# The main trip of a fused GNN and expert layer in another order on three engines

## Chip, cores and metric

One core of a Trainium2 chip. The metric is the device time of one execution in microseconds (us). The kernel before took 1512.84 us, the median of three runs (1510.32 to 1513.54).

## What is computed

The reference, cut to what matters:

```python
def layer(x, src, dst, W, b, gate_w, gate_b, w1, b1, w2, b2):   # x: 6250 x 256, 100000 edges sorted by dst
    h = layernorm(x)
    agg = segment_sum(h[src], dst) / max(degree, 1)
    out = concat([h, agg]) @ W                                   # 512 x 256
    x = x + out / norm(out) + b
    h = layernorm(x)
    probs = softmax(h @ gate_w + gate_b)                         # 8 experts
    idx, prb = argmax(probs), max(probs)
    pos = position of the node in its expert's list              # running count, in node order
    kept = pos < C                                               # C = 977
    y = relu(buf[e] @ w1[e] + b1[e]) @ w2[e] + b2[e]             # 256 -> 1024 -> 256, on the kept rows
    return x + nan_to_num(y[idx, pos] * prb * kept)
```

## The kernel before, in words

The nodes are cut into 49 blocks of 128. The edges, sorted by destination, are cut into 196 quads of 512 (four tiles of 128). A first stage (to about 135 us) normalises x, splits each value into three bf16 parts, and writes them to DRAM (`parts_d`). Then comes the main loop of 49 trips, each with four quads. The main loop is followed by trips without quads, which finish the last nodes and the last chunks of experts.

**Edge work, four times in each trip.** GpSimd (POOL) gathers the quad's source rows, one indirect DMA for each tile, into `ring`, which has room for two quads (`gather`, L460). VectorE (DVE) makes the 0/1 matrix `sel` of 128 edges by 128 nodes for four tiles (`select_quad`, L991). TensorE (PE) multiplies `sel` by the gathered rows into PSUM `ps_q` (`visit`, L684 and L690: a *visit* is four tiles for one block). DVE adds the sum of the visit before to `acc` (`add_last`, L1000). A quad that crosses from one block to the next has two visits. Since 128 nodes have some four quads of edges, there is about one such crossing in each trip, in any of its four quads.

**Node work, once in each trip, for one block.** ACT and DVE write [normalised x, mean of neighbours] to `cat` (`prepare_node`); PE transposes it (L725), ACT copies it to `cat_t` (L580), PE multiplies by the GNN weights (`linear`, L738), ACT takes the norm (L591, L515 to L517), DVE makes the new row and its mean and variance (`new_row`, L856 to L1113), then the factors of the second normalisation (`normalise_row`, L1118 to L1121). ACT normalises it (L613) and PE transposes it (`xl_transposes`, L774). In the next trip PE makes the eight gate logits (`gate`, L780), DVE chooses the expert (`route`, L1128 to L1154), PE counts the choices (`counts`, L789 and L790), and DVE works out the row's slot (`finish_row`, L1072 to L1090, which ends with the semaphore `row_ready`). POOL then scatters `row` to `disp_d`, ordered by experts (`dispatch`, L470).

**Chunk work, once in each trip from the ninth on.** It takes 128 dispatched rows of one expert through its two layers: `xc_transposes` (L731), `up` in two halves (L747), ACT's copy to `hid` (L598), `hid_transposes` (L755), ACT's relu (L604), `down` as eight products (L766), and DVE's `result` (L1210 to L1231). POOL scatters the result to the output (`results`, L478).

**What sets the order.** No scheduler does: each engine runs its own program in the order in which it is written, and semaphores tie them. On PE a table `plan` says which piece of node or chunk work follows tile 0, 1, 2 and 3 of each quad's last visit. On DVE the order is the text of its `trip`; a helper `chains` runs several dependent sequences in step, with a drain between steps. POOL's trip is the sixteen gathers of its four quads, then `dispatch`, then `results`:

```python
for k in range(QS):
    for half in range(2):
        if quads: gather(t, k, half)      # waits ring_free: the quad two before has been read
if prev:  dispatch(t, rows)               # waits row_ready >= t + 1
if chunk: results(t)                      # waits res_ready
```

The first and last node blocks of each quad (eight numbers for each trip) lie in `qtab`, and are loaded into registers once a trip: on DVE at L1252, behind the selection of quad 3, on PE at L720, behind tile 0 of quad 3.

## Time and profile before

| | |
|---|---|
| median of three runs | 1512.84 us |
| span of the profiled execution, first to last instruction | 1742.4 us |
| mean granted TensorE clock in it | 0.898 of full speed |
| busy in it: PE / PE weight loads / DVE / ACT / POOL | 1183.2 / 838.8 / 898.6 / 469.4 / 922.7 us |
| main loop, first eight trips (no chunk work) | about 135 to 351 us |
| main loop, the other 41 trips | about 351 to 1561 us |
| trips without quads | about 1561 to 1742 us |

The profiled execution has no time of its own beside its span, and this is 15% above the median of the runs. Busy is the time that an engine had an instruction in hand; PE's ends are modelled. Every row of the trace below is in the time of the profiled execution.

### The profile page before, as it was taken

How to read it: one execution, taken by the hardware profiler on the slowest of the kernel's cores; microseconds unless marked ns; L12 is line 12 of the kernel's file. 1: busy time of each engine (PE TensorE's matmuls, PEld its weight loads, DVE VectorE, ACT ScalarE, POOL GpSimd, SP SyncE). 2: the span in 40 equal slices, each digit the busy share in tenths (PEclk: the TensorE clock that was granted, in tenths of full speed). 3: DMA queues.
4: the chain of work that ended last, by engine and by line, in shares of the span. 5: the costliest groups of instructions: out<-in, count | busy, mean ns of one | idle time of the engine just before them, and what ended most of it. 6: DMA issues, size and time to landing. Idle time of an engine off the chain costs nothing.

```text
span 1742.4 us, 32300 instructions
## 1 busy us (share of the span) xinstructions
PE 1183.2 (68%) x6813; PEld 838.8 (48%) x6814; DVE 898.6 (52%) x3823; ACT 469.4 (27%) x1362; POOL 922.7 (53%) x939
## 2 busy tenths in 40 slices
PE   0105566677777777777777776877677777777785
PEld 0004444455555555555555554645455655554553
DVE  5753444455555545454555554554555545554443
ACT  2221111122222222222222322223222222233432
POOL 4136656656666656555656655565556665640110
PEclk9998676789999989998989998999998899888998
DMA  7736667554545444544445444444454544431111
GB/s 236 235 134 205 185 215 232 185 160 131 147 136 146 135 131 132 149 121 134 136 118 139 126 138 115 134 127 140 114 143 121 146 120 137 124 103 34 38 42 38
DMA packets 126810, 238.77 MB, mean 137 GB/s; under 512 B 21263, under 2 KB 85126, under 8 KB 126792
## 3 DMA queue, kind: packets, MB, share of 16 engines
q0 software_dynamic: 55808, 160.87, 32.7%
q1 hardware_dynamic: 70984, 77.72, 14.1%
q14 instruction: 14, 0.11, 0.0%
q8 instruction: 4, 0.07, 0.0%
HBM read 207.46 MB, written 39.29 MB: 142 GB/s over the span
## 4 chain that ended last, share of the span: by engine, by line
PE 28%; issue 19%; DVE 17%; another core or an unknown queue 11%; DVEq 10%; DMA 7%; ACT 4%; POOL 2%; SPq 2%; ACTq 0%; POOLq 0%
PE ps_q L684 10%; PE ps_h L747 5%; PE ps_b L766 5%; PE ps_a L738 3%; DVEq L1252 3%; DVEq L1060 2%; DMA ring<-parts_d,idx 2%; DVE sel L991 2%; PE ps_a L725 2%; DMA b_b<-in_L_ffn_b 2%; DMA out<-ys,node_i 1%; PE ps_t L755 1%; DVE acc L1000 1%; ACT cat_t L580 1%
## 5 line engine op out<-in xcount | busy, mean ns | idle before, releaser
L460 POOL DMA_INDIRECT ring<-parts_d,idx x784 | 763.0, 973 | 541.1 <-PE ps_q L684 277.9
L684 PE MATMUL ps_q<-ring,sel 128*128 128x256 bf16 x2928 | 506.0, 299 | 245.0 <-DMA ring<-parts_d,idx 96.7
L684 PEld LDWEIGHTS ps_q<-ring,sel 128*128 128x128 bf16 x2928 | 270.4, 106 | 416.8 <-issue 242.2
L766 PE MATMUL ps_b<-w_sb,hid_t 128*128 x864 | 264.6, 441 | 124.2 <-issue 71.2
L991 DVE SCALAR_TENSOR_TENSOR sel<-lane,block,dst_t 128x512 bf16<-128x512 bf16 x245 | 184.4, 753 | 197.4 <-issue 116.2
L766 PEld LDWEIGHTS ps_b<-w_sb,hid_t 128*128 128x128 f32 x864 | 169.6, 214 | 161.6 <-issue 141.5
L747 PE MATMUL ps_h<-w_sb,hid_t 128*128 x432 | 213.6, 622 | 5.7 <-ACT hid_t L583 5.7
L1000 DVE TENSOR_TENSOR acc<-acc,ps_q 128x257 f32 x245 | 103.3, 422 | 178.3 <-issue 57.3
L690 PE MATMUL ps_q<-ones_bf,sel 128*128 128x1 bf16 x976 | 170.8, 175 | 0.0
L738 PE MATMUL ps_a<-gw_sb,cat_t 128*128 128x256 f32 x416 | 136.3, 459 | 19.3 <-ACT cat_t L580 15.6
L604 ACT ACTIVATE hid_t<-ps_t,b_t 128x128 f32<-128x128 f32 x432 | 117.8, 382 | 55.5 <-remote 40.1
L515 ACT ACTIVATE sm<-sm 128x1 f32<-128x1 f32 x104 | 21.1, 203 | 358.3 <-DVE sm L1113 192.0
L690 PEld LDWEIGHTS ps_q<-ones_bf,sel 128*128 128x128 bf16 x976 | 105.0, 108 | 21.0
L478 POOL DMA_INDIRECT out<-ys,node_i x55 | 57.2, 1041 | 108.6 <-DVEq L1060 94.9
L598 ACT ACTIVATE hid<-ps_h 128x512 f32<-128x512 f32 x108 | 62.5, 596 | 193.7 <-PE ps_h L747 142.1
L470 POOL DMA_INDIRECT disp_d<-row,slot x53 | 60.2, 1136 | 90.9 <-issue 53.1
L747 PEld LDWEIGHTS ps_h<-w_sb,hid_t 128*128 128x128 f32 x432 | 76.3, 195 | 66.2 <-issue 65.2
L738 PEld LDWEIGHTS ps_a<-gw_sb,cat_t 128*128 128x128 f32 x416 | 84.0, 223 | 35.3 <-ACT cat_t L580 20.5
L755 PE MATMUL ps_t<-ident,hid 128*128 128x128 f32 x432 | 69.5, 284 | 30.0 <-ACT hid L598 25.7
L755 PEld LDWEIGHTS ps_t<-ident,hid 128*128 128x128 f32 x432 | 46.8, 141 | 46.0 <-ACT hid L598 33.3
L580 ACT ACTIVATE cat_t<-ps_a 128x512 f32<-128x512 f32 x52 | 31.0, 597 | 129.8 <-remote 64.7
L591 ACT ACTIVATE hid_t<-ps_a 128x256 f32<-128x256 f32 x52 | 19.9, 383 | 161.6 <-PE ps_a L738 91.4
(180 smaller groups left out, 1296.1 us busy)
## 6 DMA issues: line engine op xcount, KB each, us to landing
w_sb<-in_L_ffn_w SPq DMA_DIRECT2D x32, 512.0 KB
ring<-parts_d,idx POOLq DMA_INDIRECT x784
disp_d<-row SPq DMA_DIRECT2D x1, 8450.0 KB
parts_d<-w_sb SPq DMA_DIRECT2D x6, 1344.0 KB, 5.8
xs<-disp_d SPq DMA_DIRECT2D x55, 130.0 KB
ys<-disp_d SPq DMA_DIRECT2D x55, 130.0 KB
b_b<-in_L_ffn_b SPq DMA_DIRECT2D x55, 128.0 KB
xb<-in_x SPq DMA_DIRECT2D x51, 128.0 KB
```

What stands on the lines that cost most here:

```text
L460: pool.indirect_dma_start(ring[:, (k % 2) * TQ + j, :], None, parts_d[:, :], bass.IndirectOffsetOnAxis(ap=idx[:, k * TQ + j:k * TQ + j + 1 ...
L470: pool.indirect_dma_start(disp_d[:, :], bass.IndirectOffsetOnAxis(ap=slot[0:rows, 0:1], axis=0), row[0:rows, :], None, bounds_check=EX * S ...
L598: act.activation(hid[:, h * 512:(h + 1) * 512], ps_h[:, h * 512:(h + 1) * 512], ACT.Copy).then_inc(hid_ready, 1)
L604: done = act.activation(hid_t[:, j, :], ps_t[:, j, :], ACT.Relu, bias=b1_t[:, ds(e * JF + j, 1)])
L684: mm = pe.matmul(ps[:, 0:D], sel[:, s, j, :], ring[:, (k % 2) * TQ + j, part * D:(part + 1) * D], start=(j == 0 and part == 0), stop=(j == ...
L690: mm = pe.matmul(ps[:, D:AW], sel[:, s, j, :], ones_bf[:, :], start=False, stop=(j == TQ - 1), skip_group_check=True)
L738: last_ = pe.matmul(ps_a[:, 0:KD, :], cat_t[:, k, :], gw_sb[:, k, :], start=(k == 0), stop=(k == 2 * KD - 1))
L747: last_ = pe.matmul(ps_h[:, h * 512:(h + 1) * 512], xc_t[:, k, :], w1_sb[:, k, ds(expert[0] * F + h * 512, 512)], start=(k == 0), stop=(k ...
L755: last_ = pe.transpose(ps_t[:, j, :], hid[:, j * P:(j + 1) * P], ident[:, :])
L766: last_ = pe.matmul(ps_b[:, 0:D], hid_t[:, j, :], w2_sb[:, j, ds(expert[0] * D, D)], start=(j == 0), stop=(j == JF - 1))
L991: dve.scalar_tensor_tensor(out=sel[:, s, :, :], in0=lane[:, :].rearrange("p (j m) -> p j m", j=1).to_broadcast((P, TQ, P)), scalar=block0[ ...
L1000: dve.tensor_tensor(to, to, ps_q[s][:, 0:AW], ALU.add).then_inc(acc_done, 1)
```

## The change

Nothing is computed otherwise. Five things are done to the main trip.

1. PE's `plan`: `linear` (both halves), `up` 0, `up` 1 and the second half of `down` now stand behind tile 3 of quads 0, 1, 2 and 3. The `cat` transposes stand behind the gate, `xl_transposes` behind tile 1 of quad 3, `hid_transposes` 1 beside it. The trips without quads have a list of their own.
2. The loads of `qtab`: on PE behind `up` 0, into a second set of registers that is copied at the end of the trip; on DVE in two halves, behind the first step of `result` and behind the selection of quad 3.
3. DVE's trip: the logits come first of all; `new_row` comes before the sum of quad 2, `normalise_row` behind the selection of quad 3, and only then the rest of `result` with `finish_row`.
4. ACT's trip follows: the exponential of the gate comes first, relu and the copies of `hid` alternate (`hid` now holds one half), and the next node's `cat` and the copy of the normalised transposes stand at the end.
5. ACT copies `row` to a buffer `drow` when the dispatch before has landed, and POOL scatters `drow`. `new_row` no longer waits for that dispatch.

```diff
@@ gpsimd @@
-                    disp_d[:, :], ...(ap=slot[0:rows, 0:1], axis=0), row[0:rows, :], None,
+                    disp_d[:, :], ...(ap=slot[0:rows, 0:1], axis=0), drow[0:rows, :], None,
@@ scalar: the end of a trip @@
+                if chunk:
+                    hid_copy(0)
                 if node:
                     act.wait_ge(stat2_ready, t + 1)
                     act.activation(cat[:, D:2 * D], row[:, 0:D], ...).then_inc(xl_ready, 1)
+                if chunk:
+                    relu(0)
+                    hid_copy(1)
+                if node:
+                    act.wait_ge(xl_ps, t + 2)
+                    act.activation(cat_t[:, 0:KD, :], ps_a[:, 0:KD, :], ACT.Copy).then_inc(xlt_ready, 1)
+                if chunk:
+                    relu(1)
+                if node and next_node:
+                    prepare_node(t + 1, block_of(t + 1, next_known))
+                if node:
+                    act.wait_ge(disp_out, 16 * (t + 1))
+                    act.activation(drow[:, :], row[:, :], ACT.Copy).then_inc(drow_ready, 1)
@@ tensor @@
+                plan = [[steps((prev, gate), (node, cat_transposes)),
+                         steps((chunk, load_expert)),
+                         steps(),
+                         steps((node, linear, 0), (node, linear, 1))],
+                        [steps((chunk, xc_transposes)),
+                         steps(),
+                         steps(),
+                         steps((chunk, up, 0), (True, load_quads))],
+                        [steps((prev, counts)),
+                         steps((chunk, hid_transposes, 0)),
+                         steps(),
+                         steps((chunk, up, 1))],
+                        [steps(),
+                         steps((chunk, hid_transposes, 1), (node, xl_transposes)),
+                         steps((chunk, down, (0, 1, 2, 3))),
+                         steps((chunk, down, (4, 5, 6, 7)), (True, turn_quads))]]
@@ vector @@
-                dve.wait_ge(disp_out, 16 * (t + 1))
...
             def trip(...):
+                logits, routed = route(t) if prev else ([], [])
+                chains(logits)
                 if quads:
                     dve.wait_ge(cat_ready, t + 1)
                     add_last(t, 0)
                     select_quad(t, 1)
-                chains(route(t) if prev else [], choose(t, whole=prev) if chunk else [])
+                chains(routed, choose(t, whole=prev) if chunk else [])
                 if quads:
                     add_last(t, 1)
                     select_quad(t, 2)
-                chains(result(t, node) if chunk else [],
-                       ([nothing] * 3 if chunk else []) + finish_row(t) if prev else [])
+                take_y, rest = result(t, node) if chunk else (nothing, [])
+                take_y()
+                if quads:
+                    dve.load(regs[0:4], qtab[0:1, ds(t * QS + QS, QS // 2), :])
+                if node:
+                    new_row(t)
                 if quads:
                     add_last(t, 2)
                     select_quad(t, 3)
-                    dve.load(regs, qtab[0:1, ds(t * QS + QS, QS), :])
+                    dve.load(regs[4:8], qtab[0:1, ds(t * QS + QS + QS // 2, QS // 2), :])
                 if node:
-                    new_row(t)
+                    normalise_row(t)
+                else:
+                    dve.drain()
+                chains(rest, finish_row(t) if prev else [])
                 if quads:
                     add_last(t, 3)
-                if node:
-                    normalise_row(t)
-                if quads:
                     select_quad(t + 1, 0)
```

Where the rows of two engines now stand. In the rows, `[waits ...]` names the semaphores that a row waits for; ISA and REGISTER_ALU rows work on registers.

DVE at the start of a trip with chunk work. Before, behind the selection of quad 1:

```order
L991 ISA [waits visit_done]
L991 SCALAR_TENSOR_TENSOR sel<-lane,block,dst_t 128x512
L1128 TENSOR_TENSOR g<-ps_b,gateb_sb 128x8 [waits logit_ps]
L1165 SCALAR_TENSOR_TENSOR g<-seen,taken 1x8
L1131 TENSOR_REDUCE sm<-g 128x1
```

Of the change, at the head of the loop:

```order
L1308 UNCONDITIONAL_BRANCH
L1308 ISA
L1159 TENSOR_TENSOR g<-ps_b,gateb_sb 128x8 [waits logit_ps]
L1162 TENSOR_REDUCE sm<-g 128x1
L1066 ISA [waits cat_ready]
L1067 ISA [waits visit_done]
L1032 TENSOR_TENSOR acc<-acc,ps_q 128x257
```

The wait for the gate's logits moved ahead of quad 1's sum and selection.

DVE where `finish_row` begins (`g<-ps_b,seen`, which waits `count_ps`). Before, right behind the selection of quad 2 and the start of `result`:

```order
L991 SCALAR_TENSOR_TENSOR sel<-lane,block,dst_t 128x512
L1208 REGISTER_ALU [waits cat_ps]
L1209 REGISTER_ALU [waits y_ready]
L1210 TENSOR_TENSOR b_b<-ps_b,b_b 128x256 [waits ys_in]
L1213 TENSOR_SCALAR b_b<-b_b,ys 128x256
L1217 TENSOR_SCALAR cat<-b_b 128x256
L1218 TENSOR_TENSOR cat<-b_b 128x256
L1221 TENSOR_TENSOR cat<-cat 128x256
L1072 TENSOR_TENSOR g<-ps_b,seen 128x8 [waits count_ps]
```

Of the change, behind `new_row`, quad 2's sum and quad 3's selection:

```order
L1023 SCALAR_TENSOR_TENSOR sel<-lane,block,dst_t 128x512
L1290 ISA
L1290 TENSOR_LOAD qtab
L888 SCALAR_TENSOR_TENSOR sm<-sm 128x1 [waits ln2_ready]
L890 TENSOR_SCALAR sm<-sm 128x1
L1149 TENSOR_SCALAR sm<-sm 128x1
L1151 TENSOR_TENSOR row<-sm 128x1
L1152 TENSOR_TENSOR row<-sm 128x1
L1245 TENSOR_SCALAR b_b<-b_b,ys 128x256
L1104 TENSOR_TENSOR g<-ps_b,seen 128x8 [waits count_ps]
```

`finish_row` moved down by `new_row`, one sum, one selection and `normalise_row`.

POOL at the end of its trip, of the change; before, the same rows stand there with `row` for `drow` (L460 to L478):

```order
L464 DMA ring<-parts_d,idx 128x768 [waits ring_free]
L464 DMA ring<-parts_d,idx 128x768
L472 REGISTER_ALU [waits x1_out]
L474 DMA disp_d<-drow,slot 8320x260 [waits row_ready]
L480 REGISTER_ALU
L482 DMA out<-ys,node_i 6250x256 [waits res_ready]
```

Nothing moved on POOL: the next trip's first gather still stands behind both scatters.

## Rows read from the trace of the kernel before

**Rows 1.** The page: the chain that ended last, by engine.
```profile
PE 28%; issue 19%; DVE 17%; another core or an unknown queue 11%; DVEq 10%; DMA 7%; ACT 4%; POOL 2%; SPq 2%; ACTq 0%; POOLq 0%
```

**Rows 2.** Register loads by line: duration ns min/median/max, first and last start us.
```profile
L1252 DVEq TENSOR_LOAD <-qtab x49: 1457/1878/2031, 155.5 to 1551.4; - x49
L720 PEldq TENSOR_LOAD <-qtab x49: 1949/1967/2218, 156.5 to 1552.5; - x49
```

**Rows 3.** Waits in 371:1558 us: engine, line, releaser: us, times, longest.
```profile
POOL ring L460 <- PE ps_q L684: 228.5, 128, 2.7
...
PE ps_b L766 <- issue: 71.2, 42, 4.1
```

**Rows 4.** Timeline, ACT and then PE: start us, us, what [idle before <-releaser].
```profile
815.19 1.14 ACT L604 ACTIVATE hid_t<-ps_t,b_t 128x128 f32<-128x128 f32 x4 [6.65 <-remote]
...
808.60 0.66 PE L755 MATMUL ps_t<-ident,hid 128*128 128x128 f32 x4 [1.25 <-issue]
```

**Rows 5.** Timeline of DVE and POOL, 930.7 to 937 us: slot, scatters, next gathers.
```profile
930.78 0.16 DVE L1090 TENSOR_TENSOR slot<-sm 128x1 int32<-128x1 f32 x1
...
931.86 1.02 POOL L470 DMA_INDIRECT disp_d<-row,slot  x1 [0.93 <-DVE slot L1090]
...
934.49 1.17 POOL L460 DMA_INDIRECT ring<-parts_d,idx  x1 [0.30 <-issue]
935.97 1.06 POOL L460 DMA_INDIRECT ring<-parts_d,idx  x1 [0.31 <-issue]
```

**Rows 6.** Timeline: a gather (POOL) and PE's visit that waited for it.
```profile
959.56 0.94 POOL L460 DMA_INDIRECT ring<-parts_d,idx  x1 [0.30 <-DVE slot L1090]
...
962.68 0.50 PE L684 MATMUL ps_q<-ring,sel 128*128 128x256 bf16 x3 [0.30 <-DMA ring<-parts_d,idx]
```

**Rows 7.** Timeline of PE: the gate, and part of `down`.
```profile
940.04 1.11 PE L766 MATMUL ps_b<-w_sb,hid_t 128*128 x4
...
944.00 0.50 PE L684 MATMUL ps_q<-ring,sel 128*128 128x256 bf16 x3 [0.81 <-issue]
...
944.36 0.59 PE L780 MATMUL ps_b<-gatew_sb,cat_t 128*128 128x8 f32 x4
...
965.98 1.61 PE L766 MATMUL ps_b<-w_sb,hid_t 128*128 x4 [1.79 <-issue]
```

**Rows 8.** Timeline of DVE, 948 to 971 us: one trip's pieces.
```profile
948.24 0.16 DVE L1128 TENSOR_TENSOR g<-ps_b,gateb_sb 128x8 f32<-128x8 f32 x1
...
949.16 0.16 DVE L1135 RECIPROCAL sm<-sm 128x1 f32<-128x1 f32 x1 [0.40 <-issue]
...
951.94 0.42 DVE L1000 TENSOR_TENSOR acc<-acc,ps_q 128x257 f32 x1
...
953.55 0.42 DVE L1210 TENSOR_TENSOR b_b<-ps_b,b_b 128x256 f32<-128x256 f32 x1
...
957.19 0.17 DVE L1072 TENSOR_TENSOR g<-ps_b,seen 128x8 f32<-128x8 f32 x1 [1.41 <-remote]
...
959.32 0.16 DVE L1090 TENSOR_TENSOR slot<-sm 128x1 int32<-128x1 f32 x1
...
960.38 0.75 DVE L991 SCALAR_TENSOR_TENSOR sel<-lane,block,dst_t 128x512 bf16<-128x512 bf16 x1 [0.32 <-issue]
...
961.78 0.75 DVE L991 SCALAR_TENSOR_TENSOR sel<-lane,block,dst_t 128x512 bf16<-128x512 bf16 x1 [0.31 <-issue]
963.87 0.22 DVE L856 SCALAR_TENSOR_TENSOR sm<-sm 128x1 f32<-128x1 f32 x1 [1.34 <-issue]
...
966.74 0.15 DVE L1113 TENSOR_SCALAR sm<-sm 128x1 f32<-128x1 f32 x1
...
970.19 0.21 DVE L856 SCALAR_TENSOR_TENSOR sm<-sm 128x1 f32<-128x1 f32 x1
...
970.90 0.15 DVE L1121 TENSOR_TENSOR row<-sm 128x1 f32<-128x1 f32 x1
```

**Rows 9.** A stretch of the trace: us, busy by engine, granted clock, DMA.
```profile
966.50:969.80 3.30, 3.30 (x11) 2.32 (x10) 0.34 (x3) 0.40 (x2) 1.67 (x2) 0.50 0.78 203
```

More of the change, by code:

```diff
@@ L104, in gnn_moe_layer @@
         row = sb("row", [P, ROW], FP32)
+        drow = sb("drow", [P, ROW], FP32)
+        lim_t = sb("lim_t", [P, D], FP32)
         slot = sb("slot", [P, 1], I32)
@@ L414, in _ @@
             pool.memset(xb[:, :], 0.0)
+            pool.memset(drow[:, :], 0.0).then_inc(drow_ready, 1)
             pool.memset(ones_bf[:, :], 1.0).then_inc(pool_step, 1)
@@ L470, in dispatch @@
                 pool.indirect_dma_start(
-                    disp_d[:, :], bass.IndirectOffsetOnAxis(ap=slot[0:rows, 0:1], axis=0), row[0:rows, :], None,
+                    disp_d[:, :], bass.IndirectOffsetOnAxis(ap=slot[0:rows, 0:1], axis=0), drow[0:rows, :], None,
                     bounds_check=EX * SLOTS - 1, oob_is_err=False).then_inc(disp_out, 16)
@@ L559, in prepare_node, with block_of, trip, hid_copy @@
                                ).then_inc(cat_ready, 1)
-            def trip(t, node=True, prev=True, chunk=True, known=None):
-                c = chunks(t)
-                if node and known is None:
-                    act.load([blk], ntab[0:1, ds(t, 1)])
-                    known = act.snap(blk, min_val=0, max_val=NB - 2)
+            def block_of(t, known):
+                if known is None:
+                    act.load([blk], ntab[0:1, ds(t, 1)])
+                    return act.snap(blk, min_val=0, max_val=NB - 2)
+                return known
+            def trip(t, node=True, prev=True, chunk=True, next_node=True, next_known=None):
+                c = chunks(t)
+                e = None
+                def hid_copy(h):
+                    act.wait_ge(hid_ps, 2 * c - 1 + h)
+                    act.activation(hid[:, :], ps_h[:, h * 512:(h + 1) * 512],
+                                   ACT.Copy).then_inc(hid_ready, 1)
+                def relu(h):
+                    act.wait_ge(hidt_ps, 2 * c - 1 + h)
+                    for j in range(h * 4, h * 4 + 4):
+                        done = act.activation(hid_t[:, j, :], ps_t[:, j, :], ACT.Relu,
+                                              bias=b1_t[:, ds(e * JF + j, 1)])
+                    done.then_inc(hidt_ready, 1)
                 if prev:
-                    act.wait_ge(xl_ps, t + 1)
-                    act.activation(cat_t[:, 0:KD, :], ps_a[:, 0:KD, :], ACT.Copy).then_inc(xlt_ready, 1)
+                    act.wait_ge(logit_ready, t + 1)
+                    act.activation(g8[:, 1, :], g8[:, 0, :], ACT.Exp, bias=sm[:, 16:17],
+                                   accum_out=sm[:, 17:18]).then_inc(exp_ready, 1)
                 if node:
-                    prepare_node(t, known)
+                    act.wait_ge(cat_ps, t + 1)
+                    act.activation(cat_t[:, :, :], ps_a[:, :, :], ACT.Copy).then_inc(catt_ready, 1)
                 if chunk:
@@ L718, in load_quads, with turn_quads @@
                 def load_quads():
-                    pe.load(regs, qtab[0:1, ds(t * QS + QS, QS), :])
+                    pe.load(next_regs, qtab[0:1, ds(t * QS + QS, QS), :])
+                def turn_quads():
+                    for now, then in zip(regs, next_regs):
+                        pe.reg_mov(now, then)
                 def cat_transposes():
@@ new lines, in trip @@
+                        [steps(),
+                         steps((chunk, hid_transposes, 1), (node, xl_transposes)),
+                         steps((chunk, down, (0, 1, 2, 3))),
+                         steps((chunk, down, (4, 5, 6, 7)), (True, turn_quads))]]
+                alone = steps((prev, gate), (chunk, load_expert), (node, cat_transposes), (chunk, xc_transposes),
+                              (node, linear, 0), (node, linear, 1), (chunk, up, 0), (chunk, up, 1), (prev, counts),
+                              (chunk, hid_transposes, 0), (chunk, hid_transposes, 1), (node, xl_transposes),
+                              (chunk, down, tuple(range(JF))))
@@ L818, in trip @@
+                if quads:
+                    for k in range(QS):
                         quad(t, k, plan[k])
-                    else:
-                        for step in plan[k]:
-                            step()
+                else:
+                    alone()
             pe.load(regs, qtab[0:1, 0:QS, :])
@@ L1310, in _ @@
                 dve.reg_add(t_reg, t_reg, 1)
-            chains(result(dve.snap(t_reg), False))
+            take_y, rest = result(dve.snap(t_reg), False)
+            chains([take_y] + rest)
 _INS = ["x", "src", "dst", "L0_gnn_weight", "L0_gnn_bias", "L0_ffn_gate_w", "L0_ffn_gate_b",
```

71 lines of the change are left out of this document (23 added, 48 removed).

## Prediction

> **What bounds the kernel now.** I read the views in this order: the chain that ended last, the waits, then the timelines of single trips. The chain has no owner [rows 1]: PE has 28% of it, DVE with its queue 27%, and 19% is "issue", time without a visible cause. So the question is in which loop of dependences a trip closes. The main loop has 41 trips with chunk work, and they take 29.5 us each in the profiled execution ((1561 - 351) / 41, from the table).
>
> The profiled execution is 230 us longer than the median run. I read why in PE's completions: the transposes of 808.60 us and 0.66 us have released ACT only at 815.19 [rows 4], though nothing that the trace shows held PE. The matmul stood still, and engines behind it show "remote" waits. Such gaps come with the many records of PE, so I take them as made by the recording. The durations of DVE, POOL and the DMAs are not of that kind, and the sum below rests on them. Of the 230 us I give 12 to the stages outside the 41 trips, which then have 520 of their 532 us; the 41 trips have 1512.84 - 520 = 993 us without the recording, **24.2 us each**. The sum is made against this, and so against the median.
>
> Three things are near 24.2 us. POOL issues 16 gathers of 0.94 and 0.30 us between them [rows 6], and two scatters of 1.3 us, 22.5 us in all [rows 5]. It had to wait for PE to free the ring for 228.5 us in 40 trips, 5.7 us a trip [rows 3], so it runs ahead. DVE has about 23 us of work and overheads in a trip. PE has some 19 us at full clock, and stalls.
>
> **The change part by part.**
>
> *The loads.* PE's load of eight registers takes 1.97 us [rows 2], and `down` waits behind it for most of the 71.2 us that its "issue" row shows [rows 3], 1.7 us a trip. Behind `up` 0, whose four passes keep PE busy for about 1.8 us, it is nearly hidden: up to -1.7 us for PE. On DVE the load takes 1.88 us, of which 1.34 us is idle time before L856 [rows 2, 8]. Two halves of 0.94 us each, behind instructions of 0.42 and 0.75 us, leave 0.73 and 0.40 us: -0.2 us. No row has a load of four registers; between nothing saved by halving (1.88 us each, +1.7 us) and two halves fully hidden (-1.3 us) I take half the time for half the registers. The Trainium skill ("Runtime: NRT & Kernel Launch", Instruction fetch mechanics) gives such a load about 200 ns a register; the trace has 235 ns, and by the page's figure the two halves would cost 0.3 us less a trip and the total would be 11 us lower.
>
> *The long products at the end of each quad.* When a quad crosses into a new block, DVE's selection and sum stand between two visits; it now has 1.8 to 1.9 us of products beside it. That is a gain of at most 1.5 us a trip for PE, again only if PE or DVE sets the end.
>
> *The later dispatch.* This is what decides. POOL's order is not changed: gathers of trip t, dispatch, results, and only then the first gather of trip t + 1. The dispatch waits for `row_ready`, the end of `finish_row`. Before, this comes early: behind quad 2's selection. Now `new_row`, a sum, a selection, half a load and `normalise_row` stand ahead of it. And DVE's trip now begins with the wait for the gate, which PE makes behind tile 0 of quad 0, which needs the first gather. That closes a loop: slot written, dispatch, results, gather, landing, tile 0, gate, all of DVE's trip up to the slot.
>
> From the slot to the landed tiles [rows 5, 6]: slot's end 930.94 to the dispatch's start 931.86, 0.92 us; both scatters, to the next gather's start at 934.49, 2.63 us; two gathers, to 937.03, 2.54 us; landing, from a gather's end at 960.50 to the visit at 962.68, 2.18 us. Sum **8.3 us**.
>
> From the landed tiles to the slot:
> - tile 0 and gate [rows 7]: 944.00 to 944.95, and 0.1 us to DVE: 1.05 us
> - logits, route and choose [rows 8]: 948.24 to 951.94 less 0.40 us of waiting is 3.30 us. The two logit steps now run alone and the nine steps of `choose` follow; two short rounds more, 0.5 us: 3.80 us
> - three times sum and selection (quads 1, 2, 3), 951.94 to 953.55 each [rows 8]: 4.83 us
> - first step of `result`, 0.42 and a drain: 0.52 us
> - first half of the load, as above: 0.73 us
> - `new_row`, 963.87 to 966.89 [rows 8]: 3.02 us
> - second half of the load: 0.40 us
> - `normalise_row`, 970.19 to 971.05 and a drain [rows 8]: 0.96 us
> - rest of `result` with `finish_row`: 953.55 to 959.48 less the 1.41 us of waiting is 4.52 us; less the first step (0.52) and the last, behind the slot (0.6): 3.40 us
>
> Sum **18.7 us**, and the loop has 27.0 us. A crossing in quad 1, 2 or 3 adds a selection and a sum, 961.78 less 960.38, 1.4 us [rows 8]. A crossing in quad 0 adds more: the extra visit comes ahead of the gate and needs the other half of the quad, two gathers (2.5 us) and two tiles more (0.7 us), 3.2 us. With one crossing a trip the mean is 1.85 us: **28.9 us a trip**, against 24.2. PE, after the slot, has only `down` (four products in 1.9 us twice, by 1.11 us for two with overlap [rows 7]) and tile 3, about 4.2 us, so it stands still for some 4 us until the tiles land.
>
> The same account of the kernel before: slot at about 11 us of the trip instead of 19, so the loop has some 21 us, and does not bind. POOL is then ahead.
>
> *What goes with it.* DVE's wait for the last dispatch is gone (the trace shows it at nothing). ACT's copy to `drow` costs 0.6 us on an engine that is busy for 27%, and comes when the scatter has landed, 5 us after the slot, ahead of the 9 us at which ACT is next needed. ACT's relu 0 and second copy of `hid` now wait for `normalise_row`; PE's `down` waits for the slot anyway. All of these: nothing. The memset of `drow`: below 1 us, once. In the first eight trips, without `result` and the second scatter, the loop has about 24.5 us, under the 27 us that they take now: nothing, with 10 us kept for the range. The trips without quads have the same pieces in nearly the same order: nothing, within 10 us.
>
> **Sum.** 41 x (28.9 - 24.2) = 193 us, and 1512.84 + 193 = **1705 us**.
>
> The pauses also touch PE's clock. After 1.79 us without a matmul, PE has the lower of its two levels, 1.2 GHz, in 966.5 to 969.8 us (granted 0.50), and two products of `down` take 1.61 us and not 1.11 [rows 7, 9]. The Trainium skill ("TensorE: Matmul & The Clock Gate", What's actually happening) says that the throttled state is the default and that activity lifts it. By that rule tile 0 and the gate, behind a pause of 4 us each trip, would take about twice their 0.95 us, and the total would be near 1740.
>
> **The rivals.**
>
> *The ends of PE decide (faster).* If the slot came soon enough for the gathers to land by the time PE has finished `down`, PE would keep its 1.7 us from the load and part of the crossing, until DVE's 23 us and POOL's 22.5 bind: 1 us a trip, 1470 us. It decides if slot to landing (8.3 us) is no longer than the 4.2 us of PE work behind the slot, so DVE would have to reach the slot 4 us earlier than the rows say, or do its trip in 20 us less waits. For it speaks the "issue" row of `down` and that every stall named in it is on PE; against it, the fixed order of POOL. Chance 0.14.
>
> *The late completions are real in every run (a small loss).* Then all of the profile shrinks alike, by 1512.84 / 1742.4 = 0.868, and the before has 29.5 us a trip in it. The new loop has 28.9 and perhaps 2 us of late completions in it: (30.9 - 29.5) x 0.868 x 41 = 50 us, 1563 us. For it: the profile cannot tell which of its gaps the recording made. Chance 0.2.
>
> *No difference.* PE's gain and the longer loop cancel, or DVE bound both: 1513 us, chance 0.04.
>
> **How the numbers follow.** The forecast has a chance of 0.62, and its own range is 1640 to 1765: 1 us a trip either way for the cut of the rounds, the loads and the clock. The range for 8 in 10 goes from 1560, which takes in the rival of a small loss, to 1765. It leaves out the two cases at or below 1513 and a little at each end. A measurement of this kernel can tell about 0.2% (3 us) from no change. Faster by more: 0.14. Within it: 0.04. Slower by more: 0.82.
>
> **What would show it.** Right: POOL waits for DVE's slot (L1122) before the dispatch in every trip, and no longer for PE to free the ring; PE's largest wait is for the gathered tiles, some 4 us at tile 0 of quad 0, once a trip; DVE waits at the logits at the head of its trip; slot to slot is about 29 us. `down` has no "issue" wait any more. Wrong: if POOL still waits for the ring most of the time, or if PE goes from `down` straight to the next trip's tile 0, the loop does not bind.

## The result, and the profile after

The changed kernel takes **1794.18 us** in the median (1788.50 to 1795.93, 4 runs), the kernel before beside it 1511.58 us (1509.12 to 1513.54, 4 runs): 1.186 times the time, 95% interval 1.182 to 1.190, 283 us more. The forecast was 1705 us, and its range ended at 1765: the sign and the place were right, the size was not, by 89 us.

The experiments were run in five rounds, each on one chip and each with the kernel before beside them. In four of the rounds that kernel takes 1738 to 1748 us in the median, and I call these *long* rounds. In the fifth it takes 1516.79 us, and beside the result 1511.58: these are *short*. (The expectations say "a chip of 1740 us" and "a chip of 1512 us"; the last section comes back to whether it is the chip.) The profile of before has a span of 1742.4 us, as in a long round; the profile after was taken in a short one (1795.93 us, span 1793.7). So rows of before and of after can't be laid side by side for PE's ends; for DVE, POOL and the DMAs they can. Medians below are of all runs of a kernel in its round; ratios, with 95% intervals, use only the runs within 1.5% of the kernel's fastest.

The page of the changed kernel: its span, the chain that ended last by engine and by line, and two groups of section 5 (line engine op, names, count | busy, mean ns | idle before it, and what ended most of it):

```profile
span 1793.7 us, 32491 instructions
...
issue 23%; DVE 22%; DMA 17%; PE 15%; DVEq 12%; POOL 6%; ACT 3%; SPq 1%; POOLq 1%; ACTq 0%
...
L795 PE MATMUL ps_b<-w_sb,hid_t 128*128 x864 | 218.5, 400 | 0.6 <-issue 0.6
L1159 DVE TENSOR_TENSOR g<-ps_b,gateb_sb 128x8 f32<-128x8 f32 x53 | 8.8, 167 | 373.6 <-PE ps_b L809 373.6
```

In the chain of before [rows 1] PE had 28% and DMA 7%. Now DMA and POOL have 23% together, and PE 15%: the chain goes through the gathers. `down` (L795) has lost its "issue" wait of 71.2 us [rows 3], as the load of PE's registers stands elsewhere.

The waits of the main loop, 371 to 1600 us (39 trips of chunk work; engine, line, releaser: us in total, times, longest):

```profile
POOL disp_d L474 <- DVEq L1092: 327.9, 40, 9.6
DVE g L1159 <- PE ps_b L809: 315.4, 39, 8.7
...
PE ps_q L709 <- DMA ring<-parts_d,idx: 197.2, 46, 5.6
...
PE ps_t L784 <- ACT hid L577: 105.2, 78, 1.9
```

POOL hardly waits for PE to free the ring (27.4 us in all, 228.5 before [rows 3]). It stands at the dispatch for 8.2 us in every trip. Its releaser is named DVEq L1092, which is DVE's queue at the head of `finish_row`; what the dispatch waits for is `row_ready`, the slot of L1122, and it starts 0.91 to 0.92 us behind the slot's end in each of 40 trips (ninth to forty-eighth). DVE stands at the logits 8.1 us a trip, PE at the gathered tiles some 5 us. Three engines wait once a trip, each for the next: a ring.

One turn of it, from POOL's timeline, 998 to 1030 us (start us, us, line, what, [idle before <-releaser]):

```profile
998.58 1.01 POOL L474 DMA_INDIRECT disp_d<-drow,slot  x1 [8.69 <-DVEq L1092]
999.90 1.31 POOL L482 DMA_INDIRECT out<-ys,node_i  x1 [0.30 <-issue]
1001.51 0.99 POOL L464 DMA_INDIRECT ring<-parts_d,idx  x1 [0.31 <-issue]
1002.81 0.96 POOL L464 DMA_INDIRECT ring<-parts_d,idx  x1 [0.30 <-issue]
...
1029.43 1.02 POOL L474 DMA_INDIRECT disp_d<-drow,slot  x1 [7.81 <-DVEq L1092]
```

and from the timeline of PE and DVE in the same turn:

```profile
1006.72 0.82 PE L709 MATMUL ps_q<-ring,sel 128*128 128x256 bf16 x3 [4.69 <-DMA ring<-parts_d,idx]
...
1007.40 1.00 PE L809 MATMUL ps_b<-gatew_sb,cat_t 128*128 128x8 f32 x4
...
1008.45 0.17 DVE L1159 TENSOR_TENSOR g<-ps_b,gateb_sb 128x8 f32<-128x8 f32 x1 [7.76 <-PE ps_b L809]
...
1021.91 0.75 DVE L1023 SCALAR_TENSOR_TENSOR sel<-lane,block,dst_t 128x512 bf16<-128x512 bf16 x1 [1.99 <-PE ps_q L715]
...
1028.37 0.15 DVE L1122 TENSOR_TENSOR slot<-sm 128x1 int32<-128x1 f32 x1
```

This turn takes 1029.43 less 998.58, 30.85 us. Over the 41 trips with chunk work it is 31.27 us in the mean: L1159 starts at 349.10 us in the ninth trip and at 1600.03 in the forty-ninth, 40 trips later. 41 of these are 1282 us, so the rest of the program has 512 us. With about as much outside the loop in the kernel before, its trips take (1511.6 - 512) / 41 = 24.4 us where it runs in 1512 us; that is an estimate, as no trace shows that kernel in a short round.

The granted clock in three stretches of this turn (us, PE busy and its instructions, PEclk, DMA, GB/s): `down`, the pause, and tile 0 with the gate.

```profile
999.80:1002.10 2.30, 2.23 (x13) 1.00 0.05 11
1002.10:1006.70 4.60, 0.00 (x0) 0.88 0.62 179
1006.70:1009.00 2.30, 2.28 (x12) 0.50 0.60 172
```

Behind the pause of 4.7 us PE has the lower of its two levels, 1.2 GHz; tile 0 takes 0.82 us where it took 0.50, and the gate 1.00 where it took 0.59 [rows 7].

### The profile page after: what moved, and what is told of

It reads as the page before. It is cut to its first block, busy times and chain, and to the rows that moved or that the text cites. A ratio compares the mean times of both kernels' runs of the same rounds, so it can differ in the third digit from the quotient of the medians.

```text
span 1793.7 us, 32491 instructions
## 1 busy us (share of the span) xinstructions
PE 1170.5 (65%) x6813; PEld 856.1 (48%) x6814; DVE 893.6 (50%) x3823; ACT 478.3 (27%) x1414; POOL 913.6 (51%) x940
## 3 DMA queue, kind: packets, MB, share of 16 engines
q1 hardware_dynamic: 70984, 77.72, 13.2%
## 4 chain that ended last, share of the span: by engine, by line
issue 23%; DVE 22%; DMA 17%; PE 15%; DVEq 12%; POOL 6%; ACT 3%; SPq 1%; POOLq 1%; ACTq 0%
DMA ring<-parts_d,idx 13%; PE ps_q L709 7%; DVEq L1092 3%; DVEq L1290 2%; DVE sel L1023 2%; PE ps_b L809 2%; POOL ring L464 2%; DVEq L1284 2%; DMA b_b<-in_L_ffn_b 2%; PE ps_t L784 2%; POOL out L482 2%; PE ps_a L767 1%; ACT hid L577 1%; DMA out<-ys,node_i 1%; PE ps_b L795 1%
## 5 line engine op out<-in xcount | busy, mean ns | idle before, releaser
L464 POOL DMA_INDIRECT ring<-parts_d,idx x784 | 750.9, 958 | 259.6 <-issue 221.7
L1023 DVE SCALAR_TENSOR_TENSOR sel<-lane,block,dst_t 128x512 bf16<-128x512 bf16 x245 | 184.4, 752 | 196.2 <-PE ps_q L715 114.0
L474 POOL DMA_INDIRECT disp_d<-drow,slot x53 | 54.3, 1025 | 433.5 <-DVEq L1092 390.5
L795 PE MATMUL ps_b<-w_sb,hid_t 128*128 x864 | 218.5, 400 | 0.6 <-issue 0.6
L1159 DVE TENSOR_TENSOR g<-ps_b,gateb_sb 128x8 f32<-128x8 f32 x53 | 8.8, 167 | 373.6 <-PE ps_b L809 373.6
L795 PEld LDWEIGHTS ps_b<-w_sb,hid_t 128*128 128x128 f32 x864 | 162.2, 197 | 26.4 <-issue 1.3
L784 PE MATMUL ps_t<-ident,hid 128*128 128x128 f32 x432 | 71.6, 289 | 133.9 <-ACT hid L577 133.9
L767 PE MATMUL ps_a<-gw_sb,cat_t 128*128 128x256 f32 x416 | 124.6, 451 | 0.0
L784 PEld LDWEIGHTS ps_t<-ident,hid 128*128 128x128 f32 x432 | 46.6, 142 | 156.1 <-ACT hid L577 151.4
L482 POOL DMA_INDIRECT out<-ys,node_i x55 | 66.0, 1199 | 108.0 <-DVEq L1092 94.3
L767 PEld LDWEIGHTS ps_a<-gw_sb,cat_t 128*128 128x128 f32 x416 | 93.6, 238 | 16.0
L619 ACT ACTIVATE cat<-row 128x256 f32<-128x256 f32 x52 | 31.2, 601 | 254.9 <-DVEq L1153 254.9
L589 ACT ACTIVATE g<-g,sm 128x8 f32<-128x8 f32 x53 | 15.9, 300 | 304.7 <-DVE sm L1162 304.6
```

What stands on the lines that cost most here:

```text
L464: pool.indirect_dma_start(ring[:, (k % 2) * TQ + j, :], None, parts_d[:, :], bass.IndirectOffsetOnAxis(ap=idx[:, k * TQ + j:k * TQ + j + 1 ...
L474: pool.indirect_dma_start(disp_d[:, :], bass.IndirectOffsetOnAxis(ap=slot[0:rows, 0:1], axis=0), drow[0:rows, :], None, bounds_check=EX * ...
L482: pool.indirect_dma_start(out[:, :], bass.IndirectOffsetOnAxis(ap=node_i[:, 0:1], axis=0), ys[:, 0:D], None, bounds_check=N - 1, oob_is_er ...
L767: last_ = pe.matmul(ps_a[:, 0:KD, :], cat_t[:, k, :], gw_sb[:, k, :], start=(k == 0), stop=(k == 2 * KD - 1))
L784: last_ = pe.transpose(ps_t[:, j, :], hid[:, (j - 4 * h) * P:(j - 4 * h + 1) * P], ident[:, :])
L795: last_ = pe.matmul(ps_b[:, 0:D], hid_t[:, j, :], w2_sb[:, j, ds(expert[0] * D, D)], start=(j == 0), stop=(j == JF - 1))
```

## The experiments

Theory R (ring): the trip is slot, dispatch, results, gathers, landing, tile 0, gate, DVE's trip, slot, and nothing else binds. Rivals: the order on DVE or ACT is slow in itself; the loads; the clock alone. Each ratio is against the kernel before in the same round. The unaltered change was run again in a long round:

> The changed kernel unaltered, as the measure for experiments on this chip, since the kernel before took 1743 us on the chip of the first four experiments and 1512 us on another. If the slow chip is slow by a factor (1743 / 1512), the change costs 18.6% there too, above 2050 us where before takes 1743. If it is slow by late ends of matmuls that a waiting TensorE hides, the ratio is nearer 1.1 to 1.14 there. On a chip where before takes 1512 us: 1794 us.

1977.20 us against 1738.22: 1.1355 (1.1275 to 1.1436), 239 us more. The trip takes 35.05 us there (40 trips, as above) against 29.6 before. It costs 239 us here and 283 in a short round, so the long rounds still say something of the ring, by amounts of this size.

**Gathers ahead of the dispatch.** POOL's trip gathers quads 1 to 3 and then the next trip's quad 0, and only then dispatches; the wait that sat in front of them is behind them.

```diff
-    for k in range(QS): gather(t, k, half)
-    dispatch(t); results(t)
+    for k in range(1, QS): gather(t, k, half)
+    gather(t + 1, 0, half)
+    dispatch(t); results(t)
```

> The changed kernel, but POOL issues the four gathers of the next trip's quad 0 ahead of the dispatch and the results scatter. Theory (the loop slot, dispatch, results, gather, landing, tile 0, gate, DVE, slot holds each trip of 31.2 us): the gathers leave the loop, what is left is slot, down and tile 3 (4.2 us), tile 0 and gate (1.1 us), DVE to the slot (about 19.5 us), 24.8 us a trip, so about 1794 - 41 x 6.4 = 1532 us, and POOL waits for the ring again. Rival (DVE or ACT work of the new order is itself too slow, whatever POOL does): above 1740 us.

1764.27 us against 1743.22. The ratio, 0.9986 (0.9926 to 1.0045), uses only the fastest few of ten runs that spread from 1735 to 1788 us; by the medians it is 1.012. R expected 1532 us for 1512, which is 1.013, and its rival above 1.15.

> The changed kernel with the gathers ahead of the dispatch alone, again beside the unaltered change. Theory: 24.8 us a trip, 1532 us where before takes 1512; where before takes 1743 us, 1764 us as measured.

1768.93 us, 1.0185 (1.0122 to 1.0249), where the unaltered change had 1.1355 in the same round: 208 of 239 us are back.

> Gathers ahead of the dispatch, once more. If this chip runs the kernel before in 1512 us as the one of the result did, the loop's 7 us a trip go: 1500 to 1560 us, 0.99 to 1.03 times before, where the unaltered change has 1.1857. If POOL's order was only one of several reasons there, it stays above 1.06. If the chip runs the kernel before in 1740 us, 1.00 to 1.02 as measured.

A long round again: 1818.27 us, 1.0406 (1.0337 to 1.0475). The three rounds spread by more than their intervals, and this one lies above the 1.02 that I gave; between long rounds a kernel's ratio is good to some 2% and no finer.

> The change with the gathers ahead of the dispatch. On a chip of 1740 us 1.00 to 1.04 as measured; if this is a chip of 1512 us, 1500 to 1560 us if POOL's order is the whole loss, above 1.06 if it is one of several reasons.

This round ran the kernel before in 1516.79 us, and this kernel in **1558.28 us**, 1.0279 (1.0232 to 1.0326). That is just inside the 1560 us that R allows, and far from the 1794 of the unaltered change: one move on POOL takes back 236 of the 283 us (1794.18 less 1558.28, of two short rounds). R's "nothing else binds" is too strong, as 42 us stay. Its timeline, POOL and then DVE's slot and logits:

```profile
1000.83 1.02 POOL L476 DMA_INDIRECT disp_d<-drow,slot  x1 [1.93 <-DVEq L1100]
1002.15 1.32 POOL L484 DMA_INDIRECT out<-ys,node_i  x1 [0.30 <-issue]
1003.77 0.99 POOL L466 DMA_INDIRECT ring<-parts_d,idx  x1 [0.30 <-issue]
...
1023.25 1.08 POOL L466 DMA_INDIRECT ring<-parts_d,idx  x1 [0.30 <-issue]
1026.26 1.01 POOL L476 DMA_INDIRECT disp_d<-drow,slot  x1 [1.94 <-DVEq L1100]
```

```profile
999.78 0.15 DVE L1130 TENSOR_TENSOR slot<-sm 128x1 int32<-128x1 f32 x1
...
1005.12 0.17 DVE L1167 TENSOR_TENSOR g<-ps_b,gateb_sb 128x8 f32<-128x8 f32 x1 [2.17 <-PE ps_b L817]
```

From the slot's end to the logits it is 5.19 us and no longer 11.14, while from the logits to the slot both have 20.1 us (medians over the loop; in the turn above, 10.79 from 997.66 to 1008.45). The trip is 25.69 us, and both waits that DVE has left are for PE: 94.6 us in 43 trips at the logits, and 97.2 us in 41 waits at a selection. It stays 1.3 us a trip above the 24.4 of the kernel before.

**Half of it: gathers between the two scatters.** Only `results` is moved out of the ring.

> The change with the next trip's first two gathers between the dispatch and the result scatter. If the loop slot, dispatch, gathers, landing, tile 0, gate binds each trip, only the result scatter leaves it: the gathers start some 1.6 us earlier than in the unaltered change, 41 x 1.6 = 66 us, so about 1.10 times the kernel before where the unaltered change has 1.1355. If the place of the gathers only counts because POOL's whole order runs late (POOL as the bound, not the loop), it costs the same as the unaltered change or as little as with the gathers ahead of both (1.0185).

2016.54 us against 1748.05, 1.1528 (1.1478 to 1.1577). R expected 1.10. The unaltered change has 1.1355 in another round, which is within the 2% above, so this is no gain, and perhaps a loss.

> The next trip's first gathers between dispatch and result scatter, where the trace of the other chip showed the piece from slot to logits 2.9 us shorter and the piece from logits to slot 5.3 us longer, PE's completions being up to 7 us late in it. If that growth is the chip's, a chip of 1512 us shows the 1.6 us and more: 66 to 119 us less than 1794, a ratio of 1.11 to 1.14. If it belongs to the order (gathers of quad 1 behind the result scatter), 1.18 or above.

A long round once more: 2011.38 us, 1.1518 (1.1475 to 1.1560). In the traces of both the piece from slot to logits is 8.26 us and no longer 11.3, as R says, and the piece from logits to slot 27.5 and 28.8 us where the unaltered change has 23.4 in a long round (medians over 40 trips). The 3 us that the ring gives up are lost again, and more, where DVE waits for PE's ends. The waits of the first of the two (400 to 1600 us):

```profile
POOL disp_d L476 <- PE ps_q L717: 325.8, 30, 12.7
...
DVE sel L1031 <- PE ps_q L723: 163.4, 21, 9.2
```

7.8 us at each of 21 waits; in the rerun of the unaltered change the same wait has 122.4 us in 27. I put them down to the late ends that the last section shows; no run tests that. What `results` costs in the ring in a short round stays open.

**The slot earlier on DVE.** `rest` and `finish_row` ahead of `new_row`.

```diff
+    dve.drain()
+    chains(rest, finish_row(t))
     new_row(t)
     add_last(t, 2); select_quad(t, 3); ...
     normalise_row(t)
-    chains(rest, finish_row(t))
```

> The changed kernel, but DVE makes the rest of result and finish_row right behind the first step of result, as before, ahead of new_row. Theory of the loop: the slot comes 8 to 9 us earlier, the loop has about 22 us and binds no more; DVE's own work of 24 us does: about 1505 us. Rival (other moved pieces, such as ACT's waits for normalise_row or the gate at the head of the trip, carry part of the loss): 1560 to 1700 us.

1886.89 us, 1.0842 (1.0773 to 1.0910).

> The changed kernel with result and finish_row ahead of new_row alone, again, now beside the unaltered change on the same chip. Theory: within 3% of the kernel before where TensorE runs undisturbed (1480 to 1560 us where before takes 1512); where before takes 1743 us, 1887 us as measured.

1885.14 us, 1.0828 (1.0782 to 1.0874): 92 us less than the unaltered change in the same round, 2.2 us a trip. R alone expected level with the kernel before; this is its rival's range. From logits to slot it is now 13.2 us and not 23.4, from slot to logits 19.0 and not 11.3 (medians over the loop): the slot comes 10 us earlier, and 8 of these are not used. The waits of this kernel (400 to 1600 us) show what took over:

```profile
PE ps_t L784 <- issue: 337.7, 37, 11.8
ACT sm L519 <- DVE sm L1144: 272.2, 22, 14.9
```

With the slot early, `new_row` is late; ACT's first copy of `hid` (L577) stands in ACT's order behind its wait for `new_row`'s variance, and PE's transposes of `hid` (L784) wait 9 us a trip. The row names no releaser; that it is the copy is read from the same wait in the next run, where it is named.

**Both.**

> The changed kernel with both repairs: the next quad 0's gathers ahead of the dispatch, and result and finish_row ahead of new_row. Theory of the loop: no loop through POOL is left, DVE's own work of 24 us and POOL's 22.5 bind, so level with the kernel before within 3% (1480 to 1540 us where before takes 1512). Rival (the new order of ACT and of DVE's logits costs by itself): over 5% above the kernel before.

1914.66 us, 1.0999 (1.0948 to 1.1051), worse than gathers first alone in the same round (1.0185). The waits are the same pair:

```profile
ACT sm L527 <- DVE sm L1152: 430.3, 37, 14.3
...
PE ps_t L792 <- ACT hid L585: 307.5, 37, 11.1
```

**Both, and ACT's copy freed.** ACT copies `hid` ahead of its wait for the variance, and does relu 0 ahead of its wait for `normalise_row`.

```diff
+    hid_copy(0)
     act.wait_ge(var2_ready, t + 1)
     rsqrt_start(...)
-    hid_copy(0)
+    relu(0)
     act.wait_ge(stat2_ready, t + 1)
     ...
-    relu(0)
     hid_copy(1)
```

> Gathers ahead of the dispatch and the slot ahead of new_row, as in the run with both that gave 1.0999, and ACT's first copy of hid and relu 0 moved ahead of its waits for var2_ready and stat2_ready. If ACT's order was what held that run (PE waited up to 12 us for the transposes of hid), it falls to 1.02 or below. If the early slot is slow in itself (DVE's work behind it is late for PE), it stays near 1.10.

1888.49 us against 1748.05, 1.0812 (1.0782 to 1.0842). I expected 1.02 or below, and of the 1.0999 only 0.019 is gone. The copy no longer stands behind the wait for the variance, and waits for PE's `up` 0 instead, here without a named releaser (400 to 1600 us):

```profile
ACT hid L585 <- remote: 251.8, 36, 8.0
```

In long rounds ACT's order and PE's late ends can't be told apart by this pair. What holds the kernels with the early slot in a short round was not tried.

> Gathers ahead of the dispatch (1.0185 before), and the same order on ACT. In the change's trace DVE waits 2.1 us a trip at a quad's crossing for PE, which waits for ACT's copy of hid. If that wait is a term of what is left, up to 41 x 2 = 80 us go and it comes to 0.97 to 1.00; if something else stands behind it, 1.0185 again.

1799.64 us, 1.0305 (1.0274 to 1.0335).

> Gathers ahead of the dispatch, with ACT's first copy of hid and relu 0 ahead of its waits for new_row and normalise_row. If the 2.1 us a trip that DVE waits for PE at a quad's crossing come from ACT's order, up to 80 us less than with the gathers ahead alone; the chip of 1748 us showed 21 us more instead, so the rival (something else behind that wait, and the copy now in the way of ln2) expects 10 to 30 us more here too.

1800.25 us, 1.0264 (1.0209 to 1.0319). In this same round gathers first alone had 1818.27 us and 1.0406 (1.0337 to 1.0475), so ACT's order is worth 18 us here, neither the 80 of the theory nor the 10 to 30 more of its rival. The first of the two, 1.0305, has no kernel of gathers first beside it. That DVE's wait at the crossing comes from ACT's order is not confirmed as a whole.

**Logits later on DVE**, behind the sum of quad 0 and the selection of quad 1.

```diff
-    chains(logits)
     add_last(t, 0); select_quad(t, 1)
+    chains(logits)
```

> The changed kernel, but DVE makes the logit steps behind the sum and selection of quad 1, as before. Theory of the loop: that sum and selection (1.6 to 1.9 us) run while the tiles are on their way and leave the loop, 29.4 us a trip, about 1720 us. Rival (the loop does not pass through the gate): no change, 1794 us.

1970.67 us, 1.1331 (1.1261 to 1.1401), as the unaltered change (1.1355): my expectation for the theory was wrong. The work did move, into DVE's wait for the gate, but the piece from logits to slot stayed at 23.5 us (the rerun of the change: 23.4). In a long round DVE's work isn't what paces that piece: what it saves at the head it waits for further on. Beside the result the piece has 20.1 us and DVE's work fills all but some 2 of it; there the edit wasn't tried.

**PE's load alone**, in the kernel before: behind `up` 0, into registers of its own.

```diff
   # plan, quad 1:  (chunk, up, 0)           -> (chunk, up, 0), (quads, load_quads)
   # plan, quad 3:  load_quads, down (2, 3)  -> down (2, 3)
   # end of trip:   + reg_mov(now, then) for the eight registers
```

> The kernel before, with PE's load of the quads' blocks alone moved behind up 0, into second registers. If PE's stalls set the end before: 1.7 us less a trip, about 1445 us. If DVE and POOL with 23 us a trip bound it: 1480 to 1505 us. If PE's stall was covered by waits that take its place: 1512 us.

1730.59 us, 0.9939 (0.9905 to 0.9973): the part of the change that pays, 10.6 us or 0.26 us a trip, in a long round.

**PE kept busy in its pause.** Four 128x512 products into a free bank behind `down`; nothing reads them.

```diff
+    for i in range(4):
+        pe.matmul(ps_h[:, (i % 2) * 512:(i % 2 + 1) * 512], xc_t[:, 0, :], w1_sb[:, 0, 0:512],
+                  start=True, stop=True)
```

> The change with four 128x512 fp32 products (0.98 us each in the profile) whose result nothing reads, behind `down`, in PE's 4.7 us pause before tile 0. If the half clock (granted 0.50) at tile 0 and gate is a term of the loop, those two take 1.0 us and not 1.73: 41 x 0.7 = 29 us less than the unaltered change, 1.12 times before instead of 1.1355. If the clock of that stretch does not matter, 1.1355 or a little more.

1973.14 us, 1.1309 (1.1252 to 1.1366).

> Four products whose result nothing reads in PE's pause of 4.7 us. A chip of 1512 us: if the clock of tile 0 and gate is a term of 0.7 us a trip, 29 us less than the unaltered change, ratio 1.166; if not, 1.186. A chip of 1740 us: 1.13 as measured.

1976.56 us, 1.1305 (1.1258 to 1.1352). The unaltered change has 1.1355 with 1.1275 to 1.1436, in another round: the intervals overlap. In the trace of the first the products do restore the clock. In one turn, from 1000.24 us on, the granted clock is 1.00, tile 0 takes 0.50 us and the gate 0.59. Tile 0 starts no later than without them either (3.4 us behind the gathers in the median, with and without). Even so slot to logits is 12.6 us and not 11.3: DVE waits at the logits, in 29 of 35 trips without a named releaser (299.8 us). Logits to slot is 21.4 and not 23.4. So the clock comes back, and the time that it gives can't be read here, as the products also moved PE's late ends.

**A version to beat both**: the kernel before, with PE's load moved and the gathers first.

> The kernel before with PE's load behind up 0 (alone 0.9939) and POOL's first gathers of the next trip ahead of the dispatch. In the kernel before the dispatch's slot comes early and POOL waits for PE's ring instead, so the gathers' place is worth nothing or, where the dispatch now waits behind four gathers of 1.25 us and DVE's new_row waits for it, costs up to 5 us a trip: 0.99 to 1.10. Below 0.99 only if the gathers' landing was a term of the old trip.

1663.22 us against 1516.79, 1.0978 (1.0939 to 1.1016), at the upper end of what I gave. In that kernel `new_row` waits until the dispatch has landed, since POOL scatters from `row` itself, and the dispatch now stands behind four gathers. The waits of its loop (371 to 1500 us) show it:

```profile
ACT sm L523 <- DVE sm L1126: 331.4, 42, 8.8
POOL ring L462 <- PE ps_q L693: 231.2, 205, 6.5
...
DVE row L1116 <- DMA disp_d<-row,slot: 118.8, 42, 4.4
```

2.8 us a trip at `new_row` itself, of the 3.6 us (146 / 41) that it costs. So the same move is worth 236 us where the slot is late, and where it is early it costs 146, with PE's load moved as well. No version tried beats the kernel before by more than the load's 0.6%.

## Why the prediction was wrong, and where it was right

**"This is what decides": right.** The dispatch behind the late slot closes the ring; POOL stands at it in each trip, PE at tile 0, DVE at the logits. Moving the gathers past it takes back 236 of 283 us, which is the test of the cause.

**The base, "made by the recording": wrong in its reason, right in its number.** I put the 230 us by which the profile exceeded the median down to the recording. Four rounds take 1738 to 1748 us for that kernel in timed runs, with mean clocks of 0.89 to 0.91, and the trace of before has 1742.4 us and 0.898: it is an execution of that kind. A recording adds nothing: the changed kernel's profiled execution took 1795.93 us as a run and has a span of 1793.7. So PE's late ends are real in long rounds. The 24.2 us a trip for a short round has held all the same (24.4 by the estimate above), because it rests on the median run and not on that reason; that the result came from a short round as well was luck. The rival that made the late ends real in every run is out: in the trace of the result, of a short round, the copy that waits for such an end in a long one does not wait (last section), and the change costs 283 and 239 us, not 50.

**The ring's sum, 28.9 us: the step that failed.** 31.27 was measured, 2.37 us more. That is 97 us in 41 trips; less 8 us for the 24.4 in place of 24.2 before, it is the 89 us that the forecast lacks. By its own terms, with the turn at 998.58 to 1029.43 us above and the mean of 40 trips (ninth to forty-ninth, from the same trace):

| term | forecast | this turn | mean |
|---|---|---|---|
| slot to dispatch | 0.92 | 0.92 | 0.92 |
| both scatters | 2.63 | 2.93 (998.58 to 1001.51) | 2.90 |
| two gathers | 2.54 | 2.26 (to 1003.77) | 2.27 |
| landing | 2.18 | 2.95 (to 1006.72) | 3.35 |
| tile 0 and gate | 1.05 | 1.73 (to 1008.45) | 1.93 |
| DVE from the logits to the slot, crossing included | 17.65 + 1.85 = 19.50 | 20.07 (to 1028.52) | 19.91 |
| sum | 28.8 | 30.9 | 31.3 |

*Landing*, the largest miss: 1.2 us a trip. I took 2.18 us from a single gather that came late in a quad [rows 6]. Here it is 2.85 to 3.88 us. The two gathers come behind two scatters and others follow at once (DMA share 0.62 in the pause); that this is the reason is argued and not tested.

*Tile 0 and gate*: 1.73 us in 28 of the 36 trips without a crossing in quad 0, 0.7 us more than the forecast, at half clock; in four of them it is 1.0 us, the price that I took, at 0.95 to 1.00. The last 1 us ahead of DVE's logits in one trip of each sort (us, PE busy and its instructions, PEclk, DMA, GB/s):

```profile
506.01:507.01 1.00, 1.00 (x10) 1.00 0.63 180
537.66:538.66 1.00, 1.00 (x7) 0.50 0.75 227
```

The mean of 1.93 us also holds the four trips with the crossing in quad 0, 4.9 us each, which the forecast books in the last row. The prediction's own sentence on the Trainium skill ("TensorE: Matmul & The Clock Gate", What's actually happening) had this term, that the throttled state is the default and activity lifts it, and the trace agrees: granted 0.50 behind the pause, 0.82 and 1.00 us for what took 0.50 and 0.59. I had the price in that sentence and left it out of the sum; 1740 us would still have been 54 short. That filling the pause wins the time back isn't shown.

*The crossing*: its price was wrong and two other errors hid it. It falls in quad 0 in only 4 of the 40 trips, and in these DVE has 17.2 us from the logits to the slot; in the other 36 it has 20.2. So a crossing in quads 1 to 3 adds 3.0 us there and not 1.4, since DVE waits for PE's end of a visit, `sel L1023`, 1.99 us in this turn and 83.0 us over 39 trips (waits of the main loop, DVE):

```profile
DVE sel L1023 <- PE ps_q L715: 83.0, 52, 2.9
```

I had no row for it. It does not come from the ring, since the kernel with the gathers first has it too (97.2 us), where the ring is open. Ahead of that visit PE stands for 1.12 us behind the load and 1.12 us for ACT's copy of `hid` in this turn; which of these makes it late isn't shown. Against it, I had booked a crossing in quad 0 for every fourth trip, 0.3 us too much in the mean, and 0.4 us too much for the loads. Two loads of four registers:

```profile
L1284 DVEq TENSOR_LOAD <-qtab x49: 962/969/983, 142.5 to 1606.9; - x49
```

0.97 us is half of the 1.88 us for eight [rows 2], as forecast, and 0.31 and 0.41 us of them are seen ahead of L888, and not 0.73 and 0.40. The Trainium skill ("Runtime: NRT & Kernel Launch", Instruction fetch mechanics) would have a register at about 200 ns; the trace has 242 here and 235 before, so the measurement decides. That page has registers loaded from HBM, and `qtab` lies in SBUF.

**The first eight trips, the tail, ACT's copy to `drow`: nothing, right.** L1159 goes from 137.25 us in the first trip to 349.10 in the ninth, 212 us for eight (before about 216). The rest of the program has 512 us where I had 520. L633, the copy, takes 0.40 us and not 0.6, and nothing waits for it.

**PE's load: right in place, less than I allowed for.** `down` waits no more, and the kernel before gains 0.26 us a trip by it in a long round. PE is still idle for 1.12 us behind `up` 0, as the load outlasts it:

```profile
1015.26 1.96 PE L776 MATMUL ps_h<-w_sb,hid_t 128*128 x4
1018.34 0.50 PE L709 MATMUL ps_q<-ring,sel 128*128 128x256 bf16 x3 [1.12 <-issue]
```

**The range**: I gave the forecast's own range 1 us a trip either way, 41 us for terms taken each from a single row. The ring alone missed by 2.4. Its large errors (landing, clock, the wait at the crossing) have one sign: each was read from a kernel in which the engines did not stand still once a trip, or was given no row.

## What to carry to other kernels

Ask of a moved wait what stands behind it in the same in-order queue. A scatter that waits for a late result holds up all the gathers behind it, and if those feed the result, the trip becomes the sum of all the latencies; put the prefetch ahead of the wait before the result is made later. But then ask who waits for the scatter: here the same move gains 236 us in one order and goes with a loss of 146 in the other. And when a ring closes that wasn't closed before, take its terms from the worst rows and the lower clock, as its members now meet the pause.

## What the runs showed of the hardware

**The same kernel has two times, by round.** The kernel before: 1743.22, 1738.22, 1748.05 and 1748.06 us in four rounds, 1516.79 in the fifth and 1511.58 beside the result. Within a round all its runs lie within 1.5%, so the time holds for the round. That it belongs to the chip is not shown: the rounds of 1738.22 and of 1516.79 us carry the same chip number on record (0), and whether that is one chip or two of that number isn't recorded. Each kernel has a lower mean granted clock in long rounds: the kernel before 0.89 to 0.91 against 0.93 to 0.95, the change 0.83 against 0.88, gathers first 0.84 to 0.88 against 0.92 to 0.93. Whether the clock is a cause or follows from PE's standing still is open.

In long rounds single matmuls release their consumers several us late, at places that repeat each trip. From the rerun of the change there, PE and then ACT:

```profile
1017.68 0.17 PE L715 MATMUL ps_q<-ones_bf,sel 128*128 128x1 bf16 x1
1017.71 1.96 PE L776 MATMUL ps_h<-w_sb,hid_t 128*128 x4
1020.80 0.50 PE L709 MATMUL ps_q<-ring,sel 128*128 128x256 bf16 x3 [1.13 <-issue]
```

```profile
1026.44 0.60 ACT L577 ACTIVATE hid<-ps_h 128x512 f32<-128x512 f32 x1 [4.58 <-remote]
```

By its record `up` 0 ends at 1019.67, and its consumer was free from 1021.85 on; it starts at 1026.44, 6.8 us behind that end. The clock is not the reason here, as it was granted in full in the stretch where `up` 0 ends (us, PE busy and its instructions, PEclk, DMA, GB/s):

```profile
1018.00:1022.00 4.00, 2.57 (x14) 1.00 0.60 176
```

In the trace of the result the same copy starts at 1019.72, with no wait of its own, behind products recorded from 1015.26 to 1017.22. Over the whole run the copies of L577 have 82 us of "remote" waits in the long round (26 waits) and none in that trace. "remote", with no releaser, is how the profile shows such an end; the "remote" and "issue" rows in the trace of before [rows 4] look like the same thing. Why it happens in these rounds stays open. A trace whose execution is 15% above the median of the runs should first be taken as one of the other kind of execution, not as one that the recording disturbed.
